# Rotary attention: stacked rows of two head groups loaded inside the projection, and the first group's row maxima made at the projection's end

## The chip, the cores and the metric

The kernel runs on one core of a Trainium2 chip. A time is device microseconds of one launch; less is better. The times of a kernel are medians of several launches, and the profile is one further launch, taken by the hardware profiler. TensorE is called PE, VectorE DVE, ScalarE ACT, GpSimd POOL, and SyncE, which here only issues DMAs, SP.

## The reference, cut to what matters

```python
x = x + attention_a(layernorm(x), wq, wk, wv, wo)      # 1024 tokens x 512, 32 heads of 16, rotary, causal
x = x + ffn(layernorm(x), ...)                         # LoRA experts, top 2 of 8
x = x + attention_b(layernorm(x), ...)                 # 32 query heads, 8 key heads of 128
x = x + ffn(layernorm(x), ...)

def attention_a(x, wq, wk, wv, wo):
    q, k, v = heads(x @ wq.T), heads(x @ wk.T), heads(x @ wv.T)
    q, k = rotary(q), rotary(k)
    s = where(causal, q k^T * 16 ** -0.5, -1e30)
    return merge(softmax(s) @ v) @ wo.T
```

All is float32. The change touches the first line alone.

## The kernel before

The rotary attention is three blocks of engine programs; between two blocks every engine waits for all the others.

**Projection** (`rotary_projection_block`). The tokens are eight tiles of 128. LayerNorm (`LayerNorm`, lines 135 to 212) makes a normalized tile on DVE (line 183), PE turns it into one of three PSUM banks (line 204), ACT takes it out as the high part (line 211) and DVE as the low part (line 188). While the first tile is projected, PE turns the tiles 1 to 7 between the four steps of that projection. Each tile is then projected in three passes (lines 72 to 74), rotated, split into three bf16 parts, transposed (line 335) and gathered in `stage`. Every two tiles, 256 tokens called a half-pair here and numbered h = 0 to 3, SP waits for the copies of both tiles (lines 289, 290) and stores them into three DRAM tensors `parts` with six DMAs (line 294). At the end SP waits for all stores (line 297), and the block ends.

**Attention** (`rotary_attention_block`). Heads go in eight groups of four; each group has a tile `q_st` and a tile `k_st` of 96 rows (six stacks of 16) by 4 heads by 1024 tokens, in four buffers. `load` fills both with 12 DMAs (line 522). A softmax needs the row maxima first: PE makes 48 score pieces of a group (`piece`, lines 603 and 606), DVE reduces each (line 713), splits the maxima into three bf16 rows (`split_max`, lines 718 to 727), PE turns them (line 612), DVE copies them out (`take_max`, line 734), and SP writes them with three DMAs into rows 96 to 98 of `q_st` (line 529). Keys carry ones in these rows, which POOL sets with four fills of 3x4096 (line 566). For group 0 all this stands ahead of the loop, and 18 pieces of group 1 too. Then `Fori` runs twice over four groups; the scores (line 629) of a group run while the pieces of the next one are made. PE enters the loop after `ones_made` has reached four.

SP's order ahead of the loop is: the loads of group 0 in two halves by heads (24 DMAs), of group 1 (12), two of the output weight, three DMAs that copy the first two groups' rows behind the last ones in `parts` (line 540, DRAM to DRAM, so that the loop's loads can run past the end), the wait for the first maxima, their three DMAs, the wait for the copy (line 543).

**Output** (`rotary_output_block`) follows.

Of the kernel before, what the change touches and what calls it, by code (L numbers as in the profile page):

```python
# [7 lines left out]
F32 = mybir.dt.float32  # L20
# [80 lines left out]
class Weights:  # L101
# [6 lines left out]
    def __init__(self, nc, ctx, own, tag, pieces, apart=False):  # L108
        self.pieces = pieces
        self.apart = apart  # L110
        self.raw = [own.enter_context(nc.sbuf_tensor(f"{tag}_raw{k}", [P, src.shape[-1]], F32))
                    for k, (src, _, _) in enumerate(pieces)]
# [135 lines left out]
def rotary_projection_block(nc, ctx, norm, weights, xt_h, xt_l, w_h, w_l, v_all, credited, const, ps, parts_dram, x_in):  # L248
# [4 lines left out]
    with ExitStack() as own:  # L253
# [3 lines left out]
        prod = sb("prod", [P, 2, 4, C // 2])  # L257
        rot = sb("rot", [P, 2, 2 * C])
# [26 lines left out]
        def _(sp):  # L285
            start_at_one(sp, credited)
# [9 lines left out]
            for b in range(2):  # L296
                sp.wait_ge(stored[b], 16 * 6 * (NT // 4))
# [7 lines left out]
        def _(pe):  # L305
# [73 lines left out]
        def _(dve):  # L379
            norm.on_vector(dve, x_in)  # L380

# [22 lines left out]

# [10 lines left out]
A_BODY = 4  # L415
A_PARTS = 3
A_ROWS = 6 * DA
# [10 lines left out]
def rotary_attention_block(nc, ctx, v_all, o_all, wo_h, wo_l, credited, const, ps, parts_dram, wo_dram):  # L428
# [12 lines left out]
    UNITS = GA * NT  # L441

    PIECES = [(hh, i, c, span) for hh in range(GA) for i in range(NT) for c, span in enumerate(key_spans(i))]
# [4 lines left out]
    LINKS = 5  # L448
    FIRST_BANKS = (0, 1, 2, 3, 4, 5)
    PIECE_BANKS = (4, 5, 7)  # L450
    SHIFT = 6
    with ExitStack() as own:
        def sb(name, shape, dt=F32):
            return own.enter_context(nc.sbuf_tensor(f"ra_{name}", shape, dt))

        q_st = [sb(f"q_st{b}", [P, GA, T], BF16) for b in range(A_BODY)]
        k_st = [sb(f"k_st{b}", [P, GA, T], BF16) for b in range(A_BODY)]
        v4 = [sb(f"v4{b}", [P, NT, GA, 32]) for b in range(2)]
        pt = sb("pt", [P, 3, GA, 2 * W])
        mask = sb("mask", [P, P], BF16)  # L460
        part_max = sb("part_max", [P, 2, UNITS])
        row_max = sb("row_max", [P, UNITS])
        max_rest = sb("max_rest", [P, UNITS])
        max_part = sb("max_part", [P, A_PARTS, UNITS], BF16)
        max_rows = sb("max_rows", [P, P], BF16)
# [7 lines left out]
        copied = sem("copied")  # L473
        half_loaded = sem("half_loaded")
        loaded = [sem(f"loaded{b}") for b in range(A_BODY)]
        max_in = [sem(f"max_in{b}") for b in range(A_BODY)]
        made = sem("made")
# [15 lines left out]
        block = own.enter_context(nc.Block())  # L493

# [19 lines left out]
        def _(sp):  # L514
            def load(b, group, heads=slice(0, GA), done=None):

                rows = [parts_dram[a].rearrange("(n g h d) t -> n g d h t", n=2, g=NGA + 2, h=GA) for a in range(A_PARTS)]
                for s, (qa, ka) in enumerate(((0, 0), (0, 1), (0, 2), (1, 0), (1, 1), (2, 0))):
                    at = slice(s * DA, (s + 1) * DA)
                    for dst, n, a in ((q_st[b], 0, qa), (k_st[b], 1, ka)):  # L520
                        src = rows[a][n, group] if isinstance(group, int) else rows[a][n, bass.ds(group, 1)].squeeze(0)
                        sp.dma_start(dst[at, heads, :], src[:, heads, :]).then_inc(done or loaded[b], 16)
# [28 lines left out]
            for b in range(A_BODY):  # L551
                sp.wait_ge(loaded[b], 16 * 12 * (3 if b < 2 else 2))
# [33 lines left out]
        def _(pe):  # L586
            def piece(it, g, n, banks=PIECE_BANKS):
# [3 lines left out]
                first_group = isinstance(it, int) and g == 0  # L591
                if n == 0 and first_group:
                    pe.wait_ge(half_loaded, 16 * 12)
                elif n == (NP // 2 if first_group else 0):

                    pe.wait_ge(loaded[b], 16 * 12 * (it + 1 + g // A_BODY))
# [63 lines left out]
            pe.wait_ge(made, 2)  # L660
            pe.wait_ge(v4_zeroed, 4)
            for n in range(NP):
                piece(0, 0, n, FIRST_BANKS)
            turn_max(0, 0)
# [43 lines left out]
        def _(dve):  # L708
# [6 lines left out]
            def split_max(it, g):  # L715

                dve.wait_ge(piece_max, count(NP, it, g, NP))
                dve.tensor_tensor(row_max[:, :], part_max[:, 0, :], part_max[:, 1, :], ALU.max).then_inc(link, 1)
                dve.wait_ge(link, count(LINKS, it, g, 1))
                dve.tensor_scalar(max_part[:, 0, :], row_max[:, :], -1.0, None, ALU.mult).then_inc(link, 1)  # L720
                dve.wait_ge(link, count(LINKS, it, g, 2))
                dve.scalar_tensor_tensor(max_rest[:, :], row_max[:, :], -1.0, max_part[:, 0, :],
                                         ALU.mult, ALU.subtract).then_inc(link, 1)
                dve.wait_ge(link, count(LINKS, it, g, 3))
                dve.tensor_copy(max_part[:, 1, :], max_rest[:, :]).then_inc(link, 1)
                dve.wait_ge(link, count(LINKS, it, g, 4))
                dve.tensor_tensor(max_part[:, 2, :], max_rest[:, :], max_part[:, 1, :], ALU.subtract).then_inc(link, 1)

# [8 lines left out]
            dve.memset(part_max[:, 1, :], -3e38).then_inc(made, 1)  # L737
            dve.tensor_scalar(mask[:, :], const["rel"][:, SLIDE:SLIDE + P], 0.5 * NEG, NEG, ALU.is_le, ALU.mult).then_inc(made, 1)
            dve.wait_ge(made, 2)
            for n in range(NP):  # L740
                max_of_piece(0, 0, n, FIRST_BANKS)
            split_max(0, 0)
            take_max(0, 0)
            for n in range(pieces_before(SHIFT)):
                max_of_piece(0, 1, n, PIECE_BANKS)
            with dve.Fori(0, NGA // A_BODY) as it:
                for tau in range(A_BODY * S + 3):
                    g, t = tau // S, tau % S
                    if g < A_BODY:
# [3 lines left out]
                        if t == SPLIT_AT:  # L753
                            split_max(it, g + 1)
# [725 lines left out]
def hybrid_layer_kernel(nc, ins, out_dram):  # L1480
    with ExitStack() as ctx:
# [14 lines left out]
        w_norm2 = sb("w_norm2", [P, 2, DB])  # L1496
# [35 lines left out]
        with ExitStack() as rotary:  # L1532
            v_all = rotary.enter_context(nc.sbuf_tensor("v_all", [P, NT, C], F32))
            with ExitStack() as own:
                xt, parts, pieces = allocate(own, "a", [ins["wa"]])
                weights = Weights(nc, ctx, own, "a", pieces, apart=True)
                norm = LayerNorm(nc, ctx, own, "an", x, *xt, const, ps, banks=(6, 7, 5))

                with nc.Block() as block:
                    @block.sync  # L1540
                    def _(sp):
                        for name in ("ident", "rel", "trig", "slopes", "iota"):
                            sp.dma_start(const[name][:], ins[name]).then_inc(loaded, 16)
                        sp.dma_start(w_norm2[:, :, :], ins["w_norm"].partition_broadcast(P)).then_inc(loaded, 16)
                        for i in range(NT):
                            sp.dma_start(x[:, i, :], ins["x"][i * P:(i + 1) * P, :]).then_inc(x_in[i * len(x_in) // NT], 16)
                        weights.load(sp)
                        sp.wait_ge(loaded, 16 * 6)

                    @block.vector  # L1550
                    def _(dve):
                        dve.memset(const["neg_half"][:, :], -0.5)
                        dve.wait_ge(loaded, 16 * 6)
                        dve.tensor_copy(const["ident_bf"][:, :], const["ident"][:, :])
                        dve.scalar_tensor_tensor(const["w_norm"][:, :], w_norm2[:, 0, :], DB ** -0.5, w_norm2[:, 1, :],
                                                 ALU.mult, ALU.mult).then_inc(made, 1)
                        dve.wait_ge(made, 1)

                rotary_projection_block(nc, ctx, norm, weights, *xt, *parts, v_all, a_credited, const, ps,
                                        parts_dram, x_in)  # L1560
            o_all = rotary.enter_context(nc.sbuf_tensor("o_all", [P, NT, C], F32))
            wo_h = rotary.enter_context(nc.sbuf_tensor("wao_h", [P, KC, C], F32R))
# [69 lines left out]
```

## Time and profile before

| | us |
|---|---|
| median of 3 runs | 1810.41 (1809.52 to 1810.6) |
| the profiled execution: span | 1807.0 |
| projection block ends, attention block begins | 133.8 |
| first piece of group 0 on PE | 142.3 |
| first maxima copied out | 167.2 |
| first scores of the loop | 192.4 |

Busy shares of the span: PE 89%, DVE 62%, ACT 45%, POOL 25%. All times of the profile count from the start of the span. The difference between the span and the launch, about 3.4 us, is what lies around the span.

### The profile page before, as it was taken

To read this page: it belongs to the slowest core of one execution; us is meant where nothing else is said; L and a number is where in the kernel's file an instruction comes from. 1 tells how busy PE (TensorE), PEld (TensorE's weight loads), DVE (VectorE), ACT (ScalarE), POOL (GpSimd) and SP (SyncE) were. 2 spreads that over 40 slices of the span, in tenths; PEclk is the share of its full clock that TensorE was granted. 3 is DMA by queue.
4 is the path that set the end of the run, shared out by engine and by line. 5 is a ranking of instruction groups with operands and counts; after the bars stand their busy time and mean duration, and the time that the engine had idled before them with its cause. 6 is when DMAs were issued, how large, how long until landed. Compare 5 with 4: busy or idle time off the path is not lost. (4 is left out here: it accounts for less than half of the span.)

```text
span 1807.0 us, 32358 instructions
## 1 busy us (share of the span) xinstructions
PE 1601.9 (89%) x10264; PEld 1275.3 (71%) x10264; DVE 1129.4 (62%) x2719; ACT 815.2 (45%) x2197; POOL 449.9 (25%) x686
## 2 busy tenths in 40 slices
PE   3966699799986899989989989989989998999979
PEld 2742344344575788878878869878878887887867
DVE  5437577577656367466566556657656747657675
ACT  2540455455421364356257246337336535625611
POOL 3003000000102243234125116115224413513320
PEclk9985899899987999989999999999999999999989
DMA  3135442244101010010001001001001100100011
GB/s 133 36 108 103 70 49 37 37 57 52 49 7 47 1 39 22 1 32 30 1 15 48 1 8 42 13 3 48 13 2 31 30 1 23 39 1 13 1 42 48
DMA packets 39252, 60.14 MB, mean 33 GB/s; under 512 B 5878, under 2 KB 18422, under 8 KB 39030
## 3 DMA queue, kind: packets, MB, share of 16 engines
q1 hardware_dynamic: 39054, 57.65, 14.1%
q8 instruction: 105, 1.72, 0.4%
q14 instruction: 93, 0.76, 0.2%
HBM read 49.03 MB, written 9.96 MB: 33 GB/s over the span
## 5 line engine op out<-in xcount | busy, mean ns | idle before, releaser
L1449 DVE CUSTOM_DVE_ANT_0 ab_prob<-ps,ab_bias 128x128 f32<-128x128 f32 (+7 forms) x256 | 192.8, 753 | 152.6 <-issue 147.0
L713 DVE TENSOR_REDUCE ra_part_max<-ps 128x1 f32<-128x512 f32 (+1 forms) x450 | 219.5, 548 | 91.4 <-PE ps L603 47.2
L1354 ACT CAST ab_pt_h<-ps 128x512 fp32r<-128x512 f32 (+3 forms) x384 | 171.6, 482 | 180.6 <-PE ps L1246 180.3
L1461 DVE TENSOR_TENSOR ab_pt_l<-ps,ab_pt_h 128x512 fp32r<-128x512 f32 (+3 forms) x384 | 201.8, 553 | 28.8 <-ACT ab_pt_h L1354 24.4
L1359 ACT ACTIVATE ab_prob<-ab_prob,ab_neg_max 128x128 f32<-128x128 f32 (+7 forms) x256 | 199.9, 781 | 43.6 <-DVE ab_neg_max L1449 37.9
L72 PE MATMUL ps<-ab_pt_h,ab_v_h 128*128 128x256 f32 x640 | 201.2, 314 | 12.4 <-ACT ab_o_raw L1366 12.4
L701 ACT ACTIVATE ra_pt<-ps 128x1024 f32<-128x1024 f32 x128 | 130.1, 1023 | 174.5 <-PE ps L633 132.1
L1393 DVE SCALAR_TENSOR_TENSOR x<-ps,ab_recip,x 128x512 f32<-128x512 f32 x256 | 180.1, 750 | 31.7 <-PE ps L74 30.7
L1327 ACT ACTIVATE ab_squares<-ps 128x128 bf16<-128x128 f32 x320 | 83.7, 281 | 237.6 <-PE ps L74 237.6
L72 PE MATMUL ps<-b_w_h,b_xt_h 128*128 128x512 f32 (+1 forms) x512 | 177.9, 347 | 2.2 <-DVE ab_pt_l L1377 2.2
L74 PE MATMUL ps<-ab_pt_h,ab_v_l 128*128 128x256 f32 x640 | 179.8, 281 | 0.0
L73 PE MATMUL ps<-ab_pt_l,ab_v_h 128*128 128x256 f32 x640 | 179.6, 281 | 0.0
L73 PE MATMUL ps<-b_w_l,b_xt_h 128*128 128x512 f32 (+1 forms) x512 | 174.0, 340 | 0.0
L72 PE MATMUL ps<-ab_kt_h,ab_qt_h 128*128 128x512 f32 (+2 forms) x384 | 143.5, 374 | 33.9 <-issue 21.3
L1246 PE MATMUL ps<-ident,ab_prob 128*128 128x128 f32 x1152 | 172.2, 276 | 1.0
L74 PE MATMUL ps<-b_w_h,b_xt_l 128*128 128x512 f32 (+1 forms) x512 | 173.1, 338 | 0.0
L603 PE MATMUL ps<-ra_k_st,ra_q_st 96*128 96x512 bf16 (+1 forms) x450 | 133.0, 353 | 33.9 <-DMA ra_k_st<-parts 17.0
L1148 POOL TENSOR_TENSOR ab_gate_pool<-neg_half 128x1 f32<-128x1 f32 x188 | 36.6, 195 | 463.0 <-ACT ab_o_raw L1366 422.7
L1246 PEld LDWEIGHTS ps<-ident,ab_prob 128*128 128x128 f32 x1152 | 138.2, 142 | 14.8 <-DVE ab_pt_l L1461 2.9
L1154 POOL TENSOR_TENSOR ab_rms<-ab_ms_eps,neg_half 128x5 f32<-128x5 f32 x64 | 74.7, 1167 | 296.2 <-DVE ab_ms_eps L1412 296.2
L72 PEld LDWEIGHTS ps<-ab_pt_h,ab_v_h 128*128 128x128 f32 x640 | 120.6, 188 | 27.9 <-ACT ab_o_raw L1366 21.9
L73 PE MATMUL ps<-ab_kt_l,ab_qt_h 128*128 128x512 f32 (+2 forms) x384 | 138.8, 361 | 0.0
(182 smaller groups left out, 3598.1 us busy)
## 6 DMA issues: line engine op xcount, KB each, us to landing
ab_raw<-in_wqkv SPq DMA_DIRECT2D x28, 384.0 KB, 3.0
ab_raw<-in_wbo SPq DMA_DIRECT2D x32, 256.0 KB, 2.7
ra_q_st<-parts SPq DMA_DIRECT2D x54, 128.0 KB, 6.2
ra_k_st<-parts SPq DMA_DIRECT2D x54, 128.0 KB, 6.7
parts<-pa_stage SPq DMA_DIRECT2D x24, 256.0 KB, 3.3
a_raw<-in_wa SPq DMA_DIRECT2D x4, 768.0 KB, 9.7
f_raw<-in_wf SPq DMA_DIRECT2D x8, 324.0 KB, 4.0
x<-in_x SPq DMA_DIRECT2D x8, 256.0 KB, 5.6
```

What stands on the lines that cost most here:

```text
L72: pe.matmul(out, lh, rh, start=start, stop=False)
L73: pe.matmul(out, lh, rl, start=False, stop=False)
L74: return pe.matmul(out, ll, rh, start=False, stop=stop)
L603: last = pe.matmul(out, q_st[b][0:A_ROWS, hh, i * P:(i + 1) * P], k_st[b][0:A_ROWS, hh, k0:k1], start=True, stop=not last_span)
L701: act.activation(pt[:, k % 3, h, :], pair.rearrange("p a b -> p (a b)"), ACT.Exp).then_inc(exped, 1)
L713: dve.tensor_reduce(part_max[:, c, u:u + 1], ps[:, banks[n % len(banks)], 0:k1 - k0], AX.X, ALU.max).then_inc(piece_max, 1)
L1246: last = pe.transpose(ps[:, 4 + n % 3, j * P:(j + 1) * P], prob[:, v % 3, (j0 + j) * P:(j0 + j + 1) * P], const["ident"][:, :])
L1354: act.copy(pt_h[:, job % 2, s0:s0 + nb, col:col + P], ps[:, 4 + n % 3, 0:nb * P].rearrange("p (j q) -> p j q", q=P)).then_inc(pt_high, 1)
L1359: act.activation(prob[:, s % 3, 0:w], prob[:, s % 3, 0:w], ACT.Exp, bias=neg_max[:, s:s + 1], scale=-1.0, accum_out=sums[:, s:s + 1]).then ...
L1393: dve.scalar_tensor_tensor(x[:, i, :], ps[:, out_bank(n, last), :], recip[:, u:u + 1], x[:, i, :], ALU.mult, ALU.add).then_inc(added, 1)
L1449: dve.tensor_tensor_reduce(out=prob[:, s % 3, 0:w], in0=ps[:, 2 * (s % 2):2 * (s % 2) + 2, :].rearrange("p a b -> p (a b)")[:, 0:w], in1=b ...
L1461: dve.tensor_tensor(pt_l[:, job % 2, s0:s0 + nb, col:col + P], ps[:, 4 + n % 3, 0:nb * P].rearrange("p (j q) -> p j q", q=P), pt_h[:, job ...
```

## The change

Loads of the groups 0 and 1 move into the projection: after the six stores of each 256 tokens SP waits for them and issues 12 loads of group 0 and 12 of group 1, for these tokens alone. Then it copies the rows behind the last ones in `parts`, waits for the first maxima, stores them, and waits for the copy, all still in the projection's block. Group 0's pieces, ordered by query tile, its split, turn and copy-out stand at the projection's end on PE and DVE. LayerNorm has two PSUM banks instead of three. To make room, the raw weights lie in the memory of the stacked rows, the rotation's buffers in `o_all`, and the split output weight in `xt_h`. POOL's program of the attention block stays as it was.

```diff
+    def load_rows(self, sp, b, h):
+        cols = slice(2 * h * P, 2 * (h + 1) * P)
+        rows = [self.parts_dram[a].rearrange("(n g h d) t -> n g d h t", n=2, g=NGA + 2, h=GA) for a in range(A_PARTS)]
+        for s, (qa, ka) in enumerate(A_TERMS):
+            at = slice(s * DA, (s + 1) * DA)
+            for dst, n, a in ((self.q_st[b], 0, qa), (self.k_st[b], 1, ka)):
+                sp.dma_start(dst[at, :, cols], rows[a][n, b][:, :, cols]
+                             ).then_inc(self.loaded[1] if b else self.rows_in[h], 16)
...
+    def copy_rows(self, sp):
+        for a in range(A_PARTS):
+            rows = self.parts_dram[a].rearrange("(n r) t -> n r t", n=2)
+            sp.dma_start(rows[:, C:C + 2 * GA * DA, :], rows[:, 0:2 * GA * DA, :]).then_inc(self.copied, 16)
...
+    def score_pieces(self, pe):
+        pe.wait_ge(self.made, 2)
+        for n, (hh, i, c, (k0, k1)) in enumerate(A_FIRST):
+            if hh == 0 and c == 0 and i % 2 == 0:
+                pe.wait_ge(self.rows_in[i // 2], 16 * 2 * len(A_TERMS))
+            if n >= len(self.BANKS):
+                pe.wait_ge(self.credited["piece_max"], 1 + n + 1 - len(self.BANKS))
...
@@ SP in rotary_projection_block
-            for b in range(2):
-                sp.wait_ge(stored[b], 16 * 6 * (NT // 4))
+                sp.wait_ge(stored[h % 2], 16 * 6 * (h // 2 + 1))
+                if h == 0:
+
+                    sp.wait_ge(weights.w_low, KC)
+                first.load_rows(sp, 0, h)
+                first.load_rows(sp, 1, h)
+            first.copy_rows(sp)
+            first.store_max(sp)
+            first.wait_rows(sp)
@@ PE in rotary_projection_block
+            pe.wait_ge(rot_done, NT)
+            pe.wait_ge(v_done, NT)
+            first.score_pieces(pe)
+            first.turn_max(pe)
@@ DVE in rotary_projection_block
             norm.on_vector(dve, x_in)
+            first.prepare(dve)
...
             take_part(dve, dve.tensor_copy, staged_dve, NT - 1, 0)
+            first.max_of_pieces(dve)
+            first.split_max(dve)
+            first.take_max(dve)
@@ SP in rotary_attention_block
-            load(0, 0, slice(0, GA // 2), half_loaded)
-            load(0, 0, slice(GA // 2, GA))
-            load(1, 1)
             load_wo(0)
             load_wo(1)
-
-            for a in range(A_PARTS):
-                rows = parts_dram[a].rearrange("(n r) t -> n r t", n=2)
-                sp.dma_start(rows[:, C:C + 2 * GA * DA, :], rows[:, 0:2 * GA * DA, :]).then_inc(copied, 16)
-            sp.wait_ge(max_out, 1 + 1)
-            store_max(0)
-            sp.wait_ge(copied, 16 * A_PARTS)
@@ hybrid_layer_kernel
-                norm = LayerNorm(nc, ctx, own, "an", x, *xt, const, ps, banks=(6, 7, 5))
+                    norm = LayerNorm(nc, ctx, own, "an", x, xt_h, xt_l, const, ps, banks=(6, 7))
```

`prepare` is the fill and the mask that stood at the attention's start on DVE (lines 737, 738); `A_FIRST` is the list of pieces sorted by query tile.

## Rows read from the trace of the kernel before

**Rows 1.** Stretches: start:end, length, busy of each engine (instructions), PEclk, DMA share, GB/s
```profile
45.20:126.50 81.30, 71.60 (x444) 58.33 (x444) 38.40 (x56) 46.94 (x70) 0.00 (x0) 0.95 0.21 59
126.50:133.80 7.30, 0.00 (x0) 0.00 (x0) 0.00 (x0) 0.00 (x0) 0.00 (x0) 0.50 0.75 216
133.80:142.30 8.50, 0.00 (x0) 0.02 (x1) 0.51 (x2) 0.00 (x0) 8.33 (x7) 0.50 0.42 117
142.30:167.20 24.90, 19.49 (x81) 7.29 (x81) 23.76 (x54) 0.00 (x0) 8.30 (x6) 0.64 0.81 124
167.20:176.00 8.80, 7.82 (x31) 3.14 (x31) 8.08 (x17) 0.00 (x0) 0.00 (x0) 0.50 0.12 49
176.00:192.40 16.40, 0.00 (x0) 0.00 (x0) 0.38 (x2) 0.00 (x0) 0.00 (x0) 0.50 0.11 48
192.40:196.70 4.30, 4.26 (x19) 2.42 (x20) 1.72 (x4) 1.55 (x2) 0.00 (x0) 0.50 0.84 130
196.70:210.00 13.30, 12.31 (x103) 6.24 (x102) 10.89 (x23) 7.47 (x10) 0.00 (x0) 1.00 0.66 78
```

**Rows 2.** Waits, 120 to 260 us: total us, times, longest
```profile
PE ps L603 <- DMA ra_k_st<-parts: 17.0, 1, 17.0
PE ps L629 <- DMA ra_q_st<-ra_max_rows: 16.9, 1, 16.9
```

**Rows 3.** Waits of SP itself, 40 to 250 us
```profile
SPq L544 <- DMA parts<-parts: 22.3, 1, 22.3
SPq L297 <- DMA parts<-pa_stage: 2.8, 1, 2.8
```

**Rows 4.** Timeline of SP: start, us, line, what it issues; stretches of 110 to 193 us
```profile
112.02 4.12 SPq L294 DMA_DIRECT2D parts<-pa_stage  x6
...
126.46 4.12 SPq L294 DMA_DIRECT2D parts<-pa_stage  x6
...
133.80 0.35 SPq L522 DMA_DIRECT2D ra_q_st<-parts  x1
...
150.70 0.43 SPq L522 DMA_DIRECT2D ra_k_st<-parts  x1
151.16 0.90 SPq L525 DMA_DIRECT2D ra_wo_raw<-in_wao  x2
152.11 2.19 SPq L540 DMA_DIRECT2D parts<-parts  x3
167.19 2.27 SPq L529 DMA_DIRECT2D ra_q_st<-ra_max_rows  x3
...
192.15 0.37 SPq L522 DMA_DIRECT2D ra_q_st<-parts  x1
```

**Rows 5.** DMA in 40 slices: GB/s of 126 to 134 us, then of 160 to 176 us
```profile
GB/s 0 0 0 0 0 0 23 279 248 310 302 287 253 284 320 292 264 253 323 292 284 264 282 315 287 279 246 320 302 284 279 292 292 287 123 0 0 0 0 0
...
GB/s 113 102 113 282 394 604 0 0 0 0 0 328 0 0 0 0 0 328 0 0 41 17 12 335 0 18 0 0 0 328 0 0 0 0 0 328 0 0 0 0
```

**Rows 6.** Stretches, columns as in Rows 1: loads waiting in the queue
```profile
152.00:160.00 8.00, 7.69 (x31) 2.48 (x29) 8.00 (x18) 0.00 (x0) 0.00 (x0) 0.53 1.09 117
```

**Rows 7.** Timeline of POOL, 126 to 193 us
```profile
133.80 0.50 POOL L561 MEMSET ra_v<- 128x480 f32 x1 [94.56 <-POOLq L253]
...
135.02 14.20 POOL L566 MEMSET ra_k_st<- 3x4096 bf16 x4
```

**Rows 8.** Timeline of DVE in the LayerNorm, 28 to 46 us
```profile
36.78 2.74 DVE L183 TENSOR_SCALAR an_xn<-x,an_mean_var,an_rstd 128x512 f32<-128x512 f32 x1
39.44 0.68 DVE L188 TENSOR_TENSOR a_xt_l<-ps,a_xt_h 128x512 fp32r<-128x512 f32 x1
...
44.46 0.69 DVE L188 TENSOR_TENSOR a_xt_l<-ps,a_xt_h 128x512 fp32r<-128x512 f32 x1 [1.63 <-ACT a_xt_h L211]
```

**Rows 9.** Timeline of DVE, 95 to 190 us
```profile
133.88 0.50 DVE L738 TENSOR_SCALAR ra_mask<-rel 128x128 bf16<-128x128 f32 x1
142.79 22.61 DVE L713 TENSOR_REDUCE ra_part_max<-ps 128x1 f32<-128x128 f32 x48 [8.41 <-PE ps L606]
```

More of the change, by code:

```diff
@@ L101, with __init__ @@
 class Weights:
-    def __init__(self, nc, ctx, own, tag, pieces, apart=False):
+    def __init__(self, nc, ctx, own, tag, pieces, apart=False, raw=None):
         self.pieces = pieces
         self.apart = apart
-        self.raw = [own.enter_context(nc.sbuf_tensor(f"{tag}_raw{k}", [P, src.shape[-1]], F32))
-                    for k, (src, _, _) in enumerate(pieces)]
+        self.raw = raw or [own.enter_context(nc.sbuf_tensor(f"{tag}_raw{k}", [P, src.shape[-1]], F32))
+                           for k, (src, _, _) in enumerate(pieces)]
         self.raw_in = [ctx.enter_context(nc.semaphore(f"{tag}_raw_in{k}")) for k in range(len(pieces) if apart else 1)]
@@ L250, in sem, with rotary_projection_block @@
+def rotary_projection_block(nc, ctx, norm, weights, xt_h, xt_l, w_h, w_l, v_all, o_all, first, const, ps, parts_dram, x_in):
     def sem(name):
@@ L285, in _ @@
         def _(sp):
-            start_at_one(sp, credited)
+            start_at_one(sp, first.credited)
             for h in range(NT // 2):
@@ L425, in blocks_a, with rotary_attention_block @@
             "full": [(j, 0, 0), (j + 1, 0, W)]}[kind]
-def rotary_attention_block(nc, ctx, v_all, o_all, wo_h, wo_l, credited, const, ps, parts_dram, wo_dram):
+def rotary_attention_block(nc, ctx, v_all, o_all, wo_h, wo_l, first, const, ps, parts_dram, wo_dram):
+    credited = first.credited
     def sem(name):
@@ L440, in rotary_attention_block @@
     SETS = len(A_SETS)
-    UNITS = GA * NT
-    PIECES = [(hh, i, c, span) for hh in range(GA) for i in range(NT) for c, span in enumerate(key_spans(i))]
+    UNITS = A_UNITS
+    PIECES = A_PIECES
     NP = len(PIECES)
@@ L454, in sb @@
             return own.enter_context(nc.sbuf_tensor(f"ra_{name}", shape, dt))
-        q_st = [sb(f"q_st{b}", [P, GA, T], BF16) for b in range(A_BODY)]
-        k_st = [sb(f"k_st{b}", [P, GA, T], BF16) for b in range(A_BODY)]
+        q_st = first.q_st + [sb(f"q_st{b}", [P, GA, T], BF16) for b in range(2, A_BODY)]
+        k_st = first.k_st + [sb(f"k_st{b}", [P, GA, T], BF16) for b in range(2, A_BODY)]
         v4 = [sb(f"v4{b}", [P, NT, GA, 32]) for b in range(2)]
         pt = sb("pt", [P, 3, GA, 2 * W])
[L460 to L465, printed above, removed]
+        mask, part_max, max_part, max_rows = first.mask, first.part_max, first.max_part, first.max_rows
         o_rows = sb("o_rows", [P, 2, W])
@@ L472, in rotary_attention_block @@
         wo_low = sem("wo_low")
[L473 to L477, printed above, removed]
+        loaded, max_in = first.loaded, first.max_in
         piece_scored = sem("piece_scored")
@@ L514, in _, with load @@
         def _(sp):
-            def load(b, group, heads=slice(0, GA), done=None):
+            def load(b, group):
                 rows = [parts_dram[a].rearrange("(n g h d) t -> n g d h t", n=2, g=NGA + 2, h=GA) for a in range(A_PARTS)]
-                for s, (qa, ka) in enumerate(((0, 0), (0, 1), (0, 2), (1, 0), (1, 1), (2, 0))):
+                for s, (qa, ka) in enumerate(A_TERMS):
                     at = slice(s * DA, (s + 1) * DA)
                     for dst, n, a in ((q_st[b], 0, qa), (k_st[b], 1, ka)):
-                        src = rows[a][n, group] if isinstance(group, int) else rows[a][n, bass.ds(group, 1)].squeeze(0)
-                        sp.dma_start(dst[at, heads, :], src[:, heads, :]).then_inc(done or loaded[b], 16)
+                        src = rows[a][n, bass.ds(group, 1)].squeeze(0)
+                        sp.dma_start(dst[at, :, :], src).then_inc(loaded[b], 16)
             def load_wo(k):
@@ L590, in piece @@
                 b = g % A_BODY
[L591 to L596, printed above, removed]
+                if n == 0:
+                    earlier = first_loads(b) - 1 if b < 2 else 0
+                    pe.wait_ge(loaded[b], 16 * 12 * (it + 1 + g // A_BODY + earlier))
                 pe.wait_ge(piece_max, count(NP, it, g, n + 1 - len(banks)) if n >= len(banks) or g else 1)
@@ L658, in turn_rows @@
                 last.then_inc(rows_turned, 1)
-            pe.wait_ge(made, 2)
             pe.wait_ge(v4_zeroed, 4)
-            for n in range(NP):
-                piece(0, 0, n, FIRST_BANKS)
-            turn_max(0, 0)
             for n in range(pieces_before(SHIFT)):
@@ L735, in take_max @@
                                 ).then_inc(max_out, 1)
[L737 to L743, printed above, removed]
             for n in range(pieces_before(SHIFT)):
@@ L753, in _ @@
                         if t == SPLIT_AT:
-                            split_max(it, g + 1)
+                            first.split_max(dve, count(LINKS, it, g + 1, 0), count(NP, it, g + 1, NP))
                         if t == MAX_AT:
@@ L1532, in hybrid_layer_kernel @@
         with ExitStack() as rotary:
[L1533 to L1536, printed above, removed]
-                norm = LayerNorm(nc, ctx, own, "an", x, *xt, const, ps, banks=(6, 7, 5))
[L1539 to L1560, printed above, removed]
@@ new lines, in hybrid_layer_kernel, with _ @@
+            wo_h, wo_l = xt_h[:, :, 0:C], xt_h[:, :, C:2 * C]
+            with ExitStack() as held:
+                v_all = held.enter_context(nc.sbuf_tensor("v_all", [P, NT, C], F32))
+                first = FirstMaxima(nc, ctx, held, a_credited, const, ps, parts_dram)
+                w_norm2 = first.rows[:, 3, 0:4 * DB].bitcast(F32).rearrange("p (n d) -> p n d", n=2)
+                with ExitStack() as own:
+                    xt_l = own.enter_context(nc.sbuf_tensor("a_xt_l", [P, KC, T], F32R))
+                    w_h, w_l = [own.enter_context(nc.sbuf_tensor(f"a_w_{part}", [P, KC, 3 * C], F32R)) for part in "hl"]
+                    pieces = [(ins["wa"][k * P:(k + 1) * P, :], w_h[:, k, :], w_l[:, k, :]) for k in range(KC)]
+                    weights = Weights(nc, ctx, own, "a", pieces, apart=True, raw=first.raw_weights())
+                    norm = LayerNorm(nc, ctx, own, "an", x, xt_h, xt_l, const, ps, banks=(6, 7))
+                    with nc.Block() as block:
+                        @block.sync
+                        def _(sp):
+                            for name in ("ident", "rel", "trig", "slopes", "iota"):
+                                sp.dma_start(const[name][:], ins[name]).then_inc(loaded, 16)
+                            sp.dma_start(w_norm2[:, :, :], ins["w_norm"].partition_broadcast(P)).then_inc(loaded, 16)
+                            for i in range(NT):
+                                sp.dma_start(x[:, i, :], ins["x"][i * P:(i + 1) * P, :]).then_inc(x_in[i * len(x_in) // NT], 16)
+                            weights.load(sp)
+                            sp.wait_ge(loaded, 16 * 6)
+                        @block.vector
+                        def _(dve):
+                            dve.memset(const["neg_half"][:, :], -0.5)
+                            dve.wait_ge(loaded, 16 * 6)
+                            dve.tensor_copy(const["ident_bf"][:, :], const["ident"][:, :])
+                            dve.scalar_tensor_tensor(const["w_norm"][:, :], w_norm2[:, 0, :], DB ** -0.5, w_norm2[:, 1, :],
+                                                     ALU.mult, ALU.mult).then_inc(made, 1)
+                            dve.wait_ge(made, 1)
+                    rotary_projection_block(nc, ctx, norm, weights, xt_h, xt_l, w_h, w_l, v_all, o_all, first, const, ps,
+                                            parts_dram, x_in)
+                rotary_attention_block(nc, ctx, v_all, o_all, wo_h, wo_l, first, const, ps, parts_dram, ins["wao"])
```

115 lines of the change are left out of this document (90 added, 25 removed).

## Prediction

> **What bounds the kernel now.** PE is busy 89% of the span, so I looked first for where it is not. The table by stretches [rows 1] shows it: PE does nothing from 126.5 to 142.3 us, and nothing from 176.0 to 192.4 us. Then I asked the waits who ended these two gaps [rows 2]: the loads of group 0 end the first (17.0 us), and the three small DMAs with the first maxima end the second (16.9 us). Between them, from 142.3 to 167.2, DVE is busy 23.76 of 24.9 us: 48 reductions in 22.61 us [rows 9]. At face value the change removes much of this: 8.5 us of waiting for loads, and most of the maxima's 25 us, which start earlier.
>
> The second gap has to be read twice, though. SP issues the maxima at 167.19 and they land only when the loop starts; such a DMA is 24 KB. What lies in the queue is the copy of rows inside DRAM, issued at 152.11 [rows 4], and SP's own wait for it lasts 22.3 us [rows 3]. The slices of 160 to 176 us show how it runs [rows 5]: until 162.3 the queue works off loads, then one entry stands every six slices of 0.4 us, that is every 2.4 us, with 328 GB/s x 0.4 us = 131 KB, two pieces of 64 KB. The copy is 3 x 2 x 128 rows x 2 KB = 1.5 MB, so 12 such pairs: 12 x 2.4 = 29 us. It began at 162.3 and ends at 191.3; 1.1 us later PE starts the loop. So the start of the loop (192.4) hangs on when the copy starts, not on the maxima. The Trainium skill (DMA: Bandwidth & Descriptors, section on why a DMA increments its semaphore by 16) has the reason: a DMA is spread over the largest number of engines up to 16 that divides its outermost size, here 2. The trace agrees with its pairs.
>
> **The change part by part.** I follow SP, since everything it issued earlier now stands in one line with the stores.
>
> *LayerNorm with two banks.* Tile i now waits for the turning of tile i-1 rather than i-2, and turning tile i for the low part of i-2 rather than i-3. From the rows of DVE [rows 8]: the low part of tile 3 ends at 40.12, and only then can tile 5 be turned, which was turned from 39.58 before; the tiles 6 and 7 follow each 0.6 to 0.8 us later than before, and with them the low part of the last tile, which ended at 45.15 and lets the steady projection start. I take +0.8 us; the bounds are 0 (PE finds other work) and 2. `prepare` on DVE, 0.5 us [rows 9] and a small fill, falls between that low part and the first rotation, while ACT makes the products: nothing, or at most 0.6 us. Aliased buffers cost no instruction.
>
> *SP for each 256 tokens.* Six stores take 4.12 us to issue [rows 4]; the wait that now follows each time is the one that stands once before, 2.8 us [rows 3]. Then 24 loads. Before, 36 loads were issued from 133.80 to 151.13 [rows 4], 0.48 us each, in halves of 64 KB and whole ones of 128 KB alike, so I take the same for 32 KB: 24 x 0.48 = 11.6 us. Together 18.5 us. The stores before begin at 71.5, 91.76, 112.02 and 126.46, two of which are shown: 20.3 us apart, but the last only 14.4, because after it nothing is projected. So h = 0 and 1 are hidden under the projection, with 1.8 us to spare, and h = 2 is not: 112.0 + 0.8 + 18.5 = 131.3, while the last stage is ready at 127.3. The last stores start 4.0 us late.
>
> *The last 256 tokens.* Stores 131.3 to 135.4, wait to 138.2, loads to 149.8. Then the copy is issued, against 152.11 before. The queue is nearly empty: 32 KB in 0.48 us is 68 GB/s, under the 117 GB/s at which a full queue of such loads moves [rows 6]. So the copy starts about 1.0 us after its issue (the stores of 126.46 first move bytes at 127.3 [rows 5]), at 150.8, 11.5 us earlier than before. It ends at 179.8.
>
> *Group 0's maxima.* PE can start at 126.2. The pieces of the query tiles 0 to 5 are 32 of 48; with 0.08 us a piece and 1.0 ns for each of the 18,432 columns, which fits the 22.61 us, they need 13.5 us, to 139.6. The last 16 wait for the loads of h = 3 of group 0: 138.2 + 5.8 + 2.3 (as before: last issue ended at 139.9, first piece at 142.3) = 146.3, then 9.1 us, then 1.8 us for split, turn and copy-out: 157.2, against 167.2. All of it lies under the copy. The ten microseconds gained there are worth nothing.
>
> *What comes after the copy.* Here the change adds something that the diff doesn't show, because it leaves it in place. The wait for the copy is now the last of the projection's block, so the attention's block can't begin before 179.8 + 0.6 (from the copy's end at 191.3 to SP's going on, by its next issue at 192.15 [rows 4]) + 0.4 (from SP's wait, which ended at 133.4, to POOL's first fill [rows 7]) = 180.8. POOL's fills for the ones begin only there. Before, they ran from 133.80 to 149.22 [rows 7], 15.4 us under the loads and the pieces. PE waits for them ahead of the loop. Its 18 pieces of group 1, 8.7 us [rows 1], hide under them, and the loads of group 2, which come earlier now, are awaited by no one for 18 us yet. The loop starts at 180.8 + 15.4 + 0.1 = 196.3 instead of 192.4.
>
> *The loop and all behind it* have the same instructions and orders. PE runs its first 4.3 us at 0.50 of its clock, 1.2 GHz [rows 1], after 16.4 us of idle time; now it stands idle for some 5 us before, after 8.7 us of pieces during which the clock was 0.50 before as well. I take the same start; a full clock would give back 2.1 us.
>
> The sum: earlier start of the copy -11.5, fills of POOL behind it +15.4, barrier and wait-ends +1.1 - 1.1 = 0: **+3.9 us**. The profiled span becomes 1810.9, and the median 1810.41 + 3.9 = **1814.3 us**.
>
> **The rivals.** (A) *SP is no bottleneck, and the clock helps.* If loads are issued every 0.40 us, their busy time, 2 x 24 x 0.08 = 3.8 us go away, and LayerNorm may lose nothing. The loop then starts at about 192: 1810.4, no change. For it: single loads last 0.35 to 0.43 us. Against: the issue row with 36 of them.
>
> (B) *Small loads clog the queue.* A load of 32 KB has 64 pieces of 512 B, as many as one of 128 KB had of 2 KB. If pieces and not bytes count, each takes the 1.1 us that 128 KB take at 117 GB/s. Then each h takes 5.6 us of stores + 26.9 of loads = 32.5 us in the queue; from 72.3 on the four end near 202, the copy near 232, the loop starts near 248: +56 us, 1866. It decides from 0.5 us per load on, where the queue no longer keeps up with SP. Against: the stores, also of 512 B pieces, move at 280 GB/s [rows 5]. The Trainium skill (DMA: Bandwidth & Descriptors, section Bandwidth) says that transfers under 64 KB are dominated by descriptors; by that each load would cost more than its bytes, as in this rival. No row here is of such small loads.
>
> (C) *Faster.* The copy doesn't hold what I say, because alone it is quick; for example on 16 engines at 117 GB/s, 13 us. It would end at 164, the loop start at 180.5: 1798.5. It decides from a copy under 25 us on (25 + 15.4 + 1.1 after 150.8 is 192.3). Against: its pairs keep their 2.4 us for 29 us, also while the rest of the queue is empty.
>
> (D) *The change does less than it says:* the pieces wait for DVE or loads so long that the maxima end behind the copy. They would have to be 22 us later than worked out; then the price is what goes beyond 180. I put it into the upper end.
>
> **How the numbers follow.** A measurement of this kernel can tell some 0.2%, 3.6 us, from no change. My forecast, +3.9, lies at that edge, and its terms are uncertain by about 2 us (issue pace 1.5, LayerNorm 1, clock at the loop's start and the phase of later clock drops 2). Forecast (a loss of 1 to 8 us) 0.72, of it 0.5 above 3.6 us; A 0.13; B with milder forms 0.08; C 0.05; D 0.02. Slower 0.57, same 0.36, faster 0.07. The range takes the forecast's terms and most of A: 1809.5 to 1821.
>
> **What would show it right or wrong.** In the changed kernel's profile: SP's last stores issued near 131 and not 127; two-piece entries of 2.4 us from about 151 to 180; no engine but POOL at work from 190 to 196; PE's wait ahead of its first line-629 work put down to POOL; the first maxima copied out near 157. The prediction is wrong if 24 loads take under 10 or over 13 us, if the copy ends elsewhere than 178 to 183, or if POOL's fills don't stand between it and the loop.

## The result, and the profile after

The changed kernel takes 1817.66 us (median of 4 runs, 1814.17 to 1820.7) where the kernel before took 1809.97: the ratio is 1.0045, with a 95% interval of 1.0031 to 1.0059. It is slower by 7.7 us, beyond the 0.2% that can be told from no change, and inside the range given, 1809.5 to 1821; the single value, 1814.3, was 3.4 us low. The forecast loss of 3.9 us is half of the measured one. The profiled execution has a span of 1814.4 us, 7.4 more than before, and 1816.26 us in all.

The stretches of the changed kernel, with the columns of [rows 1] (start:end, length, busy time of PE, PEld, DVE, ACT, POOL, clock, DMA share, GB/s):

```profile
127.50:146.60 19.10, 10.44 (x58) 5.21 (x56) 13.49 (x32) 0.98 (x2) 0.00 (x0) 0.68 0.44 127
146.60:157.50 10.90, 5.98 (x24) 2.39 (x22) 10.26 (x22) 0.00 (x0) 0.00 (x0) 0.81 0.18 54
157.50:182.80 25.30, 0.00 (x0) 0.00 (x0) 0.02 (x1) 0.00 (x0) 0.02 (x1) 0.50 0.12 53
182.80:191.90 9.10, 7.61 (x31) 3.13 (x31) 7.35 (x16) 0.00 (x0) 8.93 (x7) 0.50 0.90 158
191.90:198.45 6.55, 0.23 (x3) 0.01 (x1) 1.11 (x3) 0.00 (x0) 6.24 (x3) 0.50 0.80 103
```

The first two rows are the gain that the change aims at: group 0's maxima are made from 127.5 on, while before PE and DVE stood still until 142.3 [rows 1]. The third row is where it goes: for 25.3 us no engine computes, and the DMA queue runs at 12% of its engines. The last row is new as well: PE idle again, POOL busy for 6.24 of 6.55 us. The waits name both (SP's own, 40 to 250 us; then PE's, 120 to 260 us):

```profile
SPq L364 <- DMA parts<-parts: 22.9, 1, 22.9
SPq L286 <- DMA parts<-pa_stage: 11.0, 4, 2.8
SPq L297 <- DVE ra_max_rows L355: 5.1, 1, 5.1
```

```profile
PE ps L704 <- POOL ra_v L666: 26.7, 1, 26.7
PE ps L730 <- POOL ra_k_st L670: 6.3, 1, 6.3
```

Line 364 is the end of the projection's block behind the wait for the copy. Line 666 is among POOL's first fills in the attention's block, which begin only with the block: PE's 26.7 us are the wait for the block. Line 670 are the fills of the ones. Where [rows 2] shows the maxima's DMAs as what ended PE's wait, it is POOL now. The timeline of SP (start, duration, line, what it issues):

```profile
72.78 4.17 SPq L406 DMA_DIRECT2D parts<-pa_stage  x6
79.74 11.48 SPq L286 DMA_DIRECT2D ra_first_rows<-parts  x24
93.35 4.15 SPq L406 DMA_DIRECT2D parts<-pa_stage  x6
...
113.92 4.17 SPq L406 DMA_DIRECT2D parts<-pa_stage  x6
120.88 11.12 SPq L286 DMA_DIRECT2D ra_first_rows<-parts  x24
132.09 4.18 SPq L406 DMA_DIRECT2D parts<-pa_stage  x6
139.03 11.12 SPq L286 DMA_DIRECT2D ra_first_rows<-parts  x24
150.20 2.20 SPq L292 DMA_DIRECT2D parts<-parts  x3
157.54 1.90 SPq L297 DMA_DIRECT2D ra_first_rows<-ra_max_rows  x3
182.77 0.84 SPq L639 DMA_DIRECT2D ra_wo_raw<-in_wao  x2
```

With no wait between them it goes from the third loads (120.88 to 132.00) to the last stores, whose data was ready some 4 us before, and it issues the copy at 150.20, against 152.11 in [rows 4]. POOL and DVE (same columns, with the idle time before an instruction in brackets):

```profile
182.78 0.50 POOL L665 MEMSET ra_v<- 128x480 f32 x1 [143.34 <-POOLq L364]
...
183.91 7.07 POOL L670 MEMSET ra_first_rows<- 3x4096 bf16 x2
191.04 7.07 POOL L670 MEMSET ra_k_st<- 3x4096 bf16 x2
```

```profile
127.68 13.52 DVE L335 TENSOR_REDUCE ra_part_max<-ps 128x1 f32<-128x128 f32 x32 [1.34 <-PE ps L315]
146.63 9.12 DVE L335 TENSOR_REDUCE ra_part_max<-ps 128x1 f32<-128x512 f32 x16 [5.43 <-PE ps L312]
...
157.29 0.22 DVE L355 COPY ra_max_rows<-ps 96x128 bf16<-96x128 bf16 x1 [0.43 <-PE ps L321]
```

The maxima are out at 157.5 instead of 167.2, ten microseconds earlier, and the loop starts at 198.45 instead of 192.44, six later.

### The profile page after: what moved, and what is told of

Same layout as the page of the kernel before. It is cut to its first block and busy times, and to the rows that moved or that the text cites. A ratio compares the mean times of both kernels' runs of the same rounds, so it can differ in the third digit from the quotient of the medians.

```text
span 1814.4 us, 32422 instructions
## 1 busy us (share of the span) xinstructions
PE 1601.9 (88%) x10264; PEld 1276.9 (70%) x10264; DVE 1129.2 (62%) x2719; ACT 815.5 (45%) x2197; POOL 449.4 (25%) x686
## 5 line engine op out<-in xcount | busy, mean ns | idle before, releaser
L810 DVE TENSOR_REDUCE ra_part_max<-ps 128x1 f32<-128x512 f32 (+3 forms) x402 | 196.9, 549 | 99.7 <-PE ps L707 71.9
L62 PE MATMUL ps<-ab_kt_h,ab_qt_l 128*128 128x512 f32 (+2 forms) x384 | 139.5, 363 | 11.7 <-issue 11.7
```

The costliest lines, as they stand in the source:

```text
L62: return pe.matmul(out, ll, rh, start=False, stop=stop)
L810: dve.tensor_reduce(part_max[:, c, u:u + 1], ps[:, banks[n % len(banks)], 0:k1 - k0], AX.X, ALU.max).then_inc(piece_max, 1)
```

## The experiments

All are read at two places: the median against the kernel before, run on the same chip, and the start of the loop in the profile (PE's first matmul with 99 rows, 192.44 in the kernel before, 198.45 in the changed one). The rows come from several chips, so medians of different rows are best compared by their ratios. The last three kernels were run once.

| kernel | median us | ratio to before (95%) | loop starts |
|---|---|---|---|
| changed, again | 1818.52 | 1.0045 (1.0028 to 1.0062) | 198.95 |
| fills beside the LayerNorm | 1813.31 | 1.0012 (1.0002 to 1.0023) | 194.48 |
| fills behind the rotation | 1809.90 | 0.9993 (0.9983 to 1.0003) | 191.21 |
| wait for the copy ahead of the loop | 1800.19 | 0.9947 (0.9930 to 0.9963) | 182.66 |
| copy in six DMAs | 1793.91 | 0.9908 (0.9889 to 0.9928) | 176.02 |
| before, copy in six DMAs | 1794.70 | 0.9911 (0.9893 to 0.9930) | 175.31 |
| copy in six, fills moved | 1787.07 | 0.9859 (0.9840 to 0.9878) | 169.32 |
| the same, group 1 later | 1780.69 | 0.9833 (0.9817 to 0.9850) | 163.33 |
| the same, padded | 1781.54 | 0.9844 (0.9825 to 0.9864) | 164.81 |
| before, two banks | 1812.08 | one run | 192.84 |
| before, 192 unused bytes | 1811.75 | one run | 191.52 |
| changed, padded | 1816.75 | one run | 197.15 |

**The wait's place.** In the changed kernel:

```diff
             first.store_max(sp)
-            first.wait_rows(sp)
@@ SP in rotary_attention_block
             load_wo(1)
+            first.wait_rows(sp)
             with sp.Fori
```

> The changed kernel, with SP's wait for the copied rows moved out of the projection's block, to just ahead of the loop in the attention's block; the copy itself is untouched. Theory: the block begins when the maxima's DMAs are issued, at about 160; the fills end at 175.3; but the maxima's DMAs lie in the queue behind the copy on its two engines, so they land at 182.4 + 1.1 and the loop starts at 183.5, 15 us earlier: near 1802.7. Rival 1 (only the barrier and the fills matter, the maxima don't queue behind the copy): the loop starts at 175.4, near 1794.6. Rival 2 (neither matters): 1817.7.

The loop starts 15.8 us earlier, the median is 1800.19. POOL's fills end at 175.2 now, but PE still waits to 182.66, and for the maxima:

```profile
PE ps L730 <- DMA ra_first_rows<-ra_max_rows: 13.4, 1, 13.4
```

Rival 1 is out: the maxima are issued at 157.36, but of their 96 pieces of 256 bytes in the trace, the first moves at 158.65 and the last at 181.73, just after the copy's last piece ends at 181.65. So the copy sets the loop's start by two ways, its own wait and the queue, and the change stacked the fills upon the first.

**The copy itself.** In the changed kernel, and likewise in the kernel before:

```diff
             rows = self.parts_dram[a].rearrange("(n r) t -> n r t", n=2)
-            sp.dma_start(rows[:, C:C + 2 * GA * DA, :], rows[:, 0:2 * GA * DA, :]).then_inc(self.copied, 16)
+            for n in range(2):
+                sp.dma_start(rows[n, C:C + 2 * GA * DA, :], rows[n, 0:2 * GA * DA, :]).then_inc(self.copied, 16)
```

> The changed kernel, with the copy inside DRAM issued as six DMAs of 128 rows instead of three of 2 x 128 rows. Theory: three DMAs with an outermost size of 2 run on two engines at 64 KB per 2.42 us, 29 us; six with an outermost size of 128 run on all sixteen and are done in under 8 us, by 160. The block begins at about 160.2, when the maxima's DMAs are issued, the four fills end at 175.5, the loop starts at 175.6, 22.9 us earlier: near 1794.8. Rival (reading and writing DRAM is what is slow, not the number of engines): the copy still takes some 29 us, 1817.7.

> The kernel before, with the copy inside DRAM issued as six DMAs of 128 rows instead of three of 2 x 128 rows. Theory: the copy starts at 162.3 behind the loads and ends by 170; the maxima are issued at 167.2 to 170.4 and land by 173; the 18 pieces of group 1 end at 176.4 and come last, so the loop starts at 176.5 instead of 192.4: 1810.0 - 15.9 = 1794. Rival (the gap of 16.4 us on PE is not the copy's): 1810.

Both medians came out within 1 us of what the theory gave, the starts of the loop 0.4 us later and 1.2 us earlier. The slices of the DMA (GB/s, 40 slices) of the kernel before with the six DMAs, 158 to 176 us in 0.45 us each, against the second line of [rows 5], and the stretch of 162 to 166 us in it (columns as in [rows 1]):

```profile
GB/s 91 137 137 96 114 100 173 369 510 446 583 510 73 583 583 473 109 0 0 0 0 0 36 17 17 2 0 18 0 159 269 155 141 105 159 132 114 100 123 173
162.00:166.00 4.00, 1.22 (x4) 0.36 (x3) 3.90 (x11) 0.00 (x0) 0.00 (x0) 0.50 0.94 393
```

Up to 162.0 these are loads; from 162.0 to 166.0 the same 1.5 MB move that took 29 us before (393 GB/s x 4.0 us), with the engines 94% busy where they were 11% busy [rows 1]. The pieces in the trace agree: before, 24 of 64 KB at 2.42 us each, 58 us of engine time on two engines; now 96 of 16 KB at 0.62 us, 59 us of engine time on sixteen. One engine is as fast as before, and the same DRAM is read and written, so the number of engines was the limit. In the changed kernel the six DMAs take from 151.9 to 158.3, at 0.76 us a piece. And these two kernels settle the question about the change: with the copy out of the way, the changed kernel takes 1793.91 and the kernel before 1794.70, with overlapping intervals, and the loop starts at 176.02 and 175.31. Made earlier or not, the first group's maxima are worth nothing as long as four fills stand behind them; the wait of 6.3 us for POOL is still there:

```profile
PE ps L731 <- POOL ra_k_st L671: 6.3, 1, 6.3
```

**The fills.** First beside the LayerNorm (there `fill_ones` waits for the split weights, `weights.w_low`), then behind the rotation, as shown; the wide copy and this together are a third kernel.

```diff
             weights.split_low(pool)
+            first.fill_ones(pool, low_done)      # two fills, for k_st[0] and k_st[1]
@@ POOL in rotary_attention_block
-            for b in range(A_BODY):
+            for b in range(2, A_BODY):
                 pool.memset(k_st[b][A_ROWS:ROWS, :, :], 1.0).then_inc(ones_made, 1)
```

> The changed kernel, with POOL's fills of the ones of the first two groups moved from the attention's block into the projection's, behind the split of the weights; two of four fills stay. Theory: in the changed kernel the loop waits for the fills (block begins at 182.8 us, four fills end at 198.1, PE starts at 198.5). With two fills left POOL is done at 191.1 and the 18 pieces of group 1, which end at 193.0, come last: the loop starts at 193.2, 5.2 us earlier, the median is near 1812.5. Rival (the loss comes from the late stores, the LayerNorm and the slower projection, and the fills only fill a wait that something else ends): the loop still starts at 198, 1817.7.

> The changed kernel, with the copy left on two engines, and the fills of the ones of the first two groups in the projection's block behind the last tile's last low part, where in the earlier run with fills they stood beside the LayerNorm. Theory: the block begins at 182.8 us as in the changed kernel, and the loop starts behind the 18 pieces and the remaining fills, at 191.8 to 193.0 instead of 198.45: 5.5 to 6.6 us less than the changed kernel run beside it. Rival (the fills' place in the projection cost nothing there, and the first run's 2.5 us were chance): the same gain as in that run, 4 us.

> The changed kernel itself, to stand beside the others on the same chip. Expected: loop start at 198 to 199 us, 1814 to 1821 as before; if its median is under 1812, the loss of 0.45% was in part this kernel's own scatter.

> The changed kernel with the copy in six DMAs of 128 rows, and with the fills of the ones of the first two groups in the projection's block, behind the last low part of the last tile (in the run with fills alone they stood behind the weights' split, where they ran beside the LayerNorm on DVE and put it back by 2.5 us). Theory: with the copy alone the block begins at 160.3 us, and PE waits 6.3 us for the fills before the loop starts at 176.0. Without two of them the 18 pieces of group 1 come last: the loop starts at 171.0, 5 us earlier, near 1789. Rival (something else, such as the landing of the maxima or the load of group 2, stands right behind the fills): the loop starts at 174 or later, 1792 or more.

The first gained 4.0 us at the loop's start and not 5.2. Its fills ran from 37.85 to 45.26, beside DVE's normalization, and stretched it: the last low part ends at 48.61 instead of 46.02, and the attention's block begins 2.5 us later. From the block on it gained 6.5. DVE, 28 to 46 us:

```profile
38.60 3.21 DVE L171 TENSOR_SCALAR an_xn<-x,an_mean_var,an_rstd 128x512 f32<-128x512 f32 x1
...
42.33 3.22 DVE L171 TENSOR_SCALAR an_xn<-x,an_mean_var,an_rstd 128x512 f32<-128x512 f32 x1
```

Such an instruction takes 0.53 us where POOL is idle and 2.74 beside POOL's split of the weights [rows 8 have the latter]. The Trainium skill (SBUF — State Buffer, section Who interferes with whom) says that DVE, in some of its modes, and GpSimd contend for a port pair, and that whichever issues first holds it for its whole instruction; `tensor_scalar` is among the operations that it names for this. The trace agrees: POOL's two fills end at 41.53 and 45.26, the two long instructions on DVE at 41.81 and 45.55. Behind the rotation the fills cost nothing, and the loop starts at 191.21, 7.7 us before the changed kernel run beside it (198.95), more than the 5.5 to 6.6 expected; the median falls by 8.6 us to that of the kernel before. Of the 7.7 us, 1.2 are not the fills': the last low part ends 1.2 us earlier in this profile (45.55 against 46.74), and the block begins 1.2 us earlier. The other 6.5 are inside the range, at its upper end: the loop starts when PE is done with the 18 pieces, about 1 us before DVE is. With the six-DMA copy the loop starts at 169.32 (171.0 expected), 6.7 us before the one with four fills. From POOL's first fill in the attention's block to the loop it is 15.7 us in all four profiles in which the four fills come last, and 9.2 us in all five with two fills. So the fills cost all of the 6.3 us that the wait shows. And here the change pays at last: with the copy and the fills mended its ratio is 0.9859, where the kernel before with the mended copy has 0.9911, and the loop starts 6.0 us before that one's; in that one PE does not wait for POOL's fills, so there they were not worth moving.

**SP's queue.** Added to the last kernel:

```diff
-                first.load_rows(sp, 1, h)
-            first.copy_rows(sp)
+                for late in {0: [0], 1: [1], 2: [], 3: [2, 3]}[h]:
+                    first.load_rows(sp, 1, late)
             first.store_max(sp)
-            first.wait_rows(sp)
@@ SP in rotary_attention_block, ahead of the loop
+            first.copy_rows(sp)
+            first.wait_rows(sp)
```

> The kernel with the six-DMA copy and the moved fills, in which SP also loads group 1's rows of the third 256 tokens only after group 0's of the fourth (12 DMAs less before the last stores), and issues the copy in the attention's block behind the maxima, ahead of the loop. Theory: in the changed kernel SP is busy with loads until 132.1 while the last stage is ready at 128, so the last stores and all behind them are 4 us late. Now the last stores are issued at 128 and group 0's last rows are there 4 us earlier, the maxima are copied out at 153.5 instead of 157.6, the block begins at 156.5 and the loop starts at 167: 4 us less than with copy and fills alone, near 1785. Rival (the stores land no earlier, or the maxima wait behind the 24 loads of group 1 that now follow): no gain against the copy and fills alone, 1789.

```profile
111.59 4.16 SPq L413 DMA_DIRECT2D parts<-pa_stage  x6
...
126.22 4.15 SPq L413 DMA_DIRECT2D parts<-pa_stage  x6
133.15 16.74 SPq L292 DMA_DIRECT2D ra_first_rows<-parts  x36
151.63 1.89 SPq L304 DMA_DIRECT2D ra_first_rows<-ra_max_rows  x3
```

The last stores come 14.6 us behind the third ones, as in the kernel before (14.4 [rows 4]), where they were 18.2 behind in the changed kernel. The maxima go out 6.0 us earlier than with copy and fills alone; 2.4 of it are a LayerNorm that was done earlier in this profile (its last low part ends at 43.75 instead of 46.13, untouched by the edit), so 3.6 are SP's, near the 4 expected. The edit also moves the copy, but that stands behind the last stores and has no share in their 3.6 us; what its move did for the rest was not run alone. The loop starts at 163.33, where 167 was expected, and the median is 1780.69 (1785 expected), 1.7% under the kernel before.

**The slower projection.** In the changed kernel a tile of the projection takes 10.29 us on average instead of 10.13: the stores of two tiles follow each other after 20.57 us instead of 20.26. Three kernels were run for it: the kernel before with two banks, the kernel before with 192 unused bytes ahead of all its tensors, and the changed kernel with 64 unused bytes ahead of `xt_l` and the split weights.

```diff
+                    pad = own.enter_context(nc.sbuf_tensor("pad", [P, 16], F32))
                     xt_l = own.enter_context(nc.sbuf_tensor("a_xt_l", [P, KC, T], F32R))
```

> The kernel before, with LayerNorm on two PSUM banks instead of three, nothing else. Theory: the low part of the last tile ends 0.8 to 0.9 us later than before (46.0 instead of 45.15 us), and the tiles of the projection follow each other every 10.13 us as before. The loop starts 0.9 us earlier or later than 192.4 + 0.9 only through the DMA queue: 1811. Rival (the two banks also slow the steady projection, which in the changed kernel has a period of 10.29 us): the period is 10.29 here too.

> The kernel before, with an unused tensor of 192 bytes per partition allocated ahead of all tensors of the rotary attention, so that they lie at other addresses, as in the changed kernel. Theory: the slower steady projection of the changed kernel (matmuls 0.235 instead of 0.230 us apart, 10.29 us a tile instead of 10.13) comes from where its operands lie, and shows here too. Rival (it comes from the loads in flight, the aliased buffers or something else that the change moved): 10.13 us a tile as before. Time: 1810 or 1811.

> The changed kernel with an unused tensor of 64 bytes per partition ahead of the low part of x and the split weights, so that these operands of the projection lie 64 bytes further. Theory: their addresses make the steady projection slower (10.29 us a tile): the period goes back to 10.13, or changes. Rival (it is not these addresses): 10.29 us as in the changed kernel.

> The kernel with the six-DMA copy behind the maxima, the moved fills and group 1's third loads late, and with the 64 bytes of padding that brought the changed kernel's projection back from 10.29 to 10.13 us a tile. Theory: the period is 10.13 here too, the loop starts 1.2 us earlier relative to the low part of the last LayerNorm tile (120.3 us behind it without the padding, 119.1 with it), the median about 1 us lower, near 1779.7, which the runs may not resolve. Rival (the SP queue or the clock takes it back): 1780.7 or more.

The first two kept 10.13 us, so the banks are not it, and 192 bytes in the kernel before do nothing. The banks did a little less than was expected of them: the last low part ends at 45.72 instead of 45.15, 0.6 us later and not 0.8. In the last two the 64 bytes bring 10.13 back. The starts of the two transpositions behind the second and third projected tile on PE, in the changed kernel and then in the padded one:

```profile
64.90 1.07 PE L454 MATMUL ps<-ident_bf,pa_part 128*128 128x128 bf16 x16
75.16 1.07 PE L454 MATMUL ps<-ident_bf,pa_part 128*128 128x128 bf16 x16
```

```profile
64.51 1.07 PE L454 MATMUL ps<-ident_bf,pa_part 128*128 128x128 bf16 x16
74.64 1.07 PE L454 MATMUL ps<-ident_bf,pa_part 128*128 128x128 bf16 x16
```

10.26 us against 10.13 here; over the whole stage the changed kernel has 10.26 to 10.33, the padded one 10.13 or 10.14. The matmuls of the projection follow each other every 0.233 us instead of 0.227. In the padded kernel the loop starts 151.1 us behind the last low part and in the changed one 152.4 (152.2 in its second run), so the slower projection is worth 1.1 to 1.3 us of the 6.0 by which the changed kernel's loop is late. In the padded kernel with group 1 later the loop starts 118.4 us behind the last low part instead of 119.6, the 1.2 us expected, but the medians, 1781.54 and 1780.69, don't show it. The padding moves every tensor that is allocated behind it, so which of the operands, and what about its address, slows the matmuls is open.

## Why the prediction was right, and where it was short

*What bounds the start of the loop: right.* The two readings of the gap at 176 us, that the copy and not the maxima ends it, and that the copy lasts 29 us on its own because it uses two engines, were the base of everything; the six-DMA kernels show both. (A DMA of the maxima is 8 KB, the three together 24; the prediction has 24 for one. Nothing was worked out from it.)

*SP's line: right.* Hidden for h = 0 and 1, 4 us late for the last stores (132.09, 131.3 predicted), the copy issued at 150.20 (149.8). The sizes inside are off against each other: 24 loads took 11.1 to 11.5 us instead of 11.6, and the projection was 1.1 us slower up to the third stores, which I had not seen coming.

*LayerNorm: right in size, and partly by luck.* Its last low part ends at 46.02; 45.15 + 0.8 predicted. The two banks alone give 0.6; and over the nine profiles of kernels with this LayerNorm and nothing new beside it, this moment lies between 43.8 and 46.7.

*The copy: its start was mis-sized.* I gave it 1.0 + 29 us from its issue, and 0.6 for SP to go on, 30.6 together. It was 32.2: SP's wait ends at 182.4. The slices of 150 to 166 us show why, in GB/s of 0.4 us each (the bytes of a piece stand in the slice in which it starts):

```profile
GB/s 51 67 77 0 328 0 0 0 0 0 0 0 164 164 0 0 0 0 164 164 0 0 18 16 2 346 0 0 0 0 0 328 0 0 0 0 0 328 0 0
```

The first pair starts at 151.8 and ends at 155.2 and 155.4, 5.0 us or more after the issue at 150.20, instead of 1.0 + 2.4 us. From there on a pair comes every 2.4 us as before, and the last ends at 182.0. In the kernel before, where the copy stood in the queue behind loads, the first pair took 2.4 us like the others. Why it takes 3.4 to 3.7 us here is open.

*The fills: right in place and size, and this was the part that the diff did not show.* 182.78 to 198.11, 15.3 us (15.4 predicted), with PE's wait put down to POOL, as written. Moving two of four takes the wait away.

*The sum.* The loop starts 6.0 us later, 3.9 predicted: 1.6 of the missing 2.1 us are the start of the copy, 0.4 its later issue (the slower projection less SP's quicker loads), 0.1 the rest. That the issue time came out so close is luck in part: the projection's slower pace, 1.1 us up to the third stores, was a term that the sum did not have, and quicker loads took 0.7 of it back.

*Behind the loop's start: a term left out of the sum.* I put 2 us of uncertainty on the clock and nothing in the value. The span grew by 7.4, not 6.0. By stretches with the same work, first kernel before, then changed, the loop's first part and the output block:

```profile
192.44:215.50 23.06, 21.69 (x151) 9.98 (x152) 16.78 (x38) 12.82 (x14) 0.00 (x0) 0.91 0.54 69
482.00:511.00 29.00, 24.93 (x120) 20.29 (x120) 15.58 (x33) 6.67 (x11) 8.23 (x6) 1.00 0.16 52
```

```profile
198.45:222.10 23.65, 22.25 (x151) 10.33 (x152) 16.78 (x38) 12.82 (x14) 1.35 (x4) 0.88 0.00 1
489.50:520.00 30.50, 27.01 (x120) 21.82 (x120) 15.67 (x33) 6.91 (x12) 7.68 (x6) 0.92 0.12 43
```

The clock granted in them fell from 0.91 to 0.88 and from 1.00 to 0.92, and they got longer by 0.6 and 1.5 us; the stretch between them grew by 0.9, and 1.6 came back behind 575. That the clock's drops fall elsewhere when all is shifted by 6 us was put beforehand as noise of either sign; no run isolates it. The part behind the loop's start, nearly the same work in all fourteen profiles that this document draws on, took between 1612.3 and 1619.1 us, with 1614.6 in the kernel before and 1616.0 in the changed one, so 1.4 us lie inside the scatter and stay unassigned.

*The signs named beforehand held:* 24 loads took 11.1 to 11.5 us (10 to 13 allowed), the copy ended at 182.0 (178 to 183), and POOL's fills stood between it and the loop.

*The rivals.* A (SP no bottleneck) is out: 24 loads never took under 11.1 us. B (small loads clog the queue) is out: they landed 1.8 us after their issue in the median. The rule that transfers under 64 KB are dominated by descriptors (DMA: Bandwidth & Descriptors, section Bandwidth, in the Trainium skill) cost nothing here at 32 KB, since SP's issue was slower than the queue. C (a quick copy) is false for this kernel, yet its mechanism is what the six DMAs make: 1793.9, and not 1798.5, because on 16 engines the copy needs 6.3 us there and not 13. It is over at 158.3, when the maxima have just been issued (157.83), and no longer sets when the block ends. D is out: the maxima were out at 157.5, as predicted (157.2).

## What to carry to other kernels

Before work is moved ahead of a wait, ask what ends last there: here a copy on two of sixteen engines held both the wait and the queue, and one line that cuts it otherwise brought 0.9% to the kernel before (ratio 0.9911) and 1.4% to the changed one (from 1.0045 to 0.9908). Work moved ahead of a wait pays only when the wait and what stands behind it are gone: the same change lost 0.45% with the slow copy, was worth nothing with the quick one, and gained 0.5% once two fills were out of the way as well. A wait moved into an earlier block also moves the barrier, and with it all that other engines did under its cover; work that is left where it was can become the critical path. A DMA queue issued in order is a resource of its own, and the step that is ready early (group 1's loads) must not stand ahead of the one that is awaited.

## What was not expected of the hardware

The projection ran 1.5% slower in the changed kernel's memory layout, and 64 bytes of padding undid it (10.29 and 10.13 us a tile); 192 bytes in the kernel before changed nothing. Two fills of only three partitions on POOL, 7.4 us together, stretched two DVE instructions from 0.53 to 3.2 us each. And the first piece of a copy inside DRAM took 5.0 us from the issue on, where each further one took 2.4.
